# Eight-field to nine-field lookup and four-sample Gram products in a DLRM tower

## The reference

```python
combined = jnp.concatenate([dense_features[:, None, :], sparse_features], axis=1)
interactions = jnp.einsum('bfd,bgd->bfg', combined, combined)
iu, ju = jnp.triu_indices(27, k=1)
z = jnp.concatenate([dense_features, interactions[:, iu, ju]], axis=1)
h = jnp.concatenate([z, r_dense_features], axis=1)
h = jnp.maximum(h @ W_top1 + b_top1, 0.0)     # 607 -> 512
h = jnp.maximum(h @ W_top2 + b_top2, 0.0)     # 512 -> 256
y = h @ W_top3                                # 256 -> 1
```

## Time and profile before

| | before |
|---|---|
| median of 3 runs | 425.8 us (423.31 to 425.89) |
| span of the profiled execution | 704.5 us |
| mean granted TensorE clock in it | 0.741 |
| PE matmul busy | 384.2 us, 55% |
| DVE, ACT busy | 204.7 us, 135.2 us |
| POOL busy | 279.3 us, 40% |

### The profile page before, as it was taken

One profiled execution on the slowest core, in us unless ns is written; L12 is line 12 of the kernel. 1 busy time (PEld: TensorE's weight loads), 2 busy tenths in 40 slices (PEclk: granted clock), 3 DMA queues, 4 the chain that ended last, 5 costly groups with the idle time before them and its releaser, 6 DMA issues.

```text
span 704.5 us, 14426 instructions
## 1 busy us (share of the span) xinstructions
PE 384.2 (55%) x6049; PEld 340.9 (48%) x6049; DVE 204.7 (29%) x684; ACT 135.2 (19%) x265; POOL 279.3 (40%) x292
## 2 busy tenths in 40 slices
PE   0325428253727718295372954559364691648967
PEld 0325317152717707194361943449253581537856
DVE  0507227032304323062030710307112162304312
ACT  1104203021202202031120312114020231103421
POOL 6760452617370363605455053530727217270000
PEclk9957859775857958598585875759766696758987
DMA  4421422413023311133111331113302233013030
GB/s 135 161 84 67 130 68 60 115 40 81 22 56 55 94 53 27 48 68 92 34 30 45 68 96 30 45 34 69 102 20 54 44 75 87 23 53 54 24 46 17
DMA packets 43149, 44.14 MB, mean 63 GB/s; under 512 B 31028, under 2 KB 36028, under 8 KB 42126
## 3 DMA queue, kind: packets, MB, share of 16 engines
q1 hardware_dynamic: 33910, 24.91, 13.8%
q0 software_dynamic: 9216, 18.89, 10.9%
HBM read 38.12 MB, written 5.65 MB: 62 GB/s over the span
## 4 chain that ended last, share of the span: by engine, by line
PE 43%; issue 36%; DVE 6%; another core or an unknown queue 5%; SPq 3%; ACT 3%; DMA 3%; ACTq 0%; DVEq 0%
PE ps_g L339 13%; PE ps_o L314 13%; PE ps_m L353 11%; DVE onehot L647 5%; PE ps_t L325 4%; DMA h<-small_tables 2%; ACT emb L523 1%; SPq L258 1%; PE ps_m L380 1%; SPq L236 1%; ACT emb L514 1%; PE ps_o L397 1%; DMA x<-interaction_scratch 1%; DVE tbl_lo L638 1%
## 5 line engine op out<-in xcount | busy, mean ns | idle before, releaser
L287 POOL DMA_INDIRECT rows<-tables,idx x288 | 279.1, 969 | 355.0 <-DMA idx<-gather_ids 271.8
L647 DVE TENSOR_SCALAR onehot<-oh_ids,rownum 125x256 fp32r<-125x256 int32 x512 | 144.8, 357 | 318.1 <-PE ps_o L314 189.0
L339 PE MATMUL ps_g<-emb 128*32 128x27 f32 x4096 | 94.5, 209 | 199.0 <-issue 194.5
L339 PEld LDWEIGHTS ps_g<-emb 128*32 128x32 f32 x4096 | 70.9, 125 | 225.6 <-issue 220.5
L314 PE MATMUL ps_o<-onehot,tbl_hi 125*128 125x256 f32 x512 | 141.2, 310 | 66.1 <-DVE onehot L647 30.2
L314 PEld LDWEIGHTS ps_o<-onehot,tbl_hi 125*128 125x128 f32 x512 | 106.2, 207 | 73.2 <-issue 32.1
L314 PE MATMUL ps_o<-onehot,tbl_lo 125*128 125x256 f32 x512 | 135.0, 298 | 2.7 <-issue 2.7
L314 PEld LDWEIGHTS ps_o<-onehot,tbl_lo 125*128 125x128 f32 x512 | 106.3, 208 | 2.3 <-issue 2.3
L533 ACT ACTIVATE inter<-ps_g 128x432 f32<-128x432 f32 x32 | 17.0, 531 | 276.9 <-remote 157.6
L514 ACT ACTIVATE emb<-ps_o 128x256 f32<-128x256 f32 x64 | 38.9, 727 | 122.5 <-PE ps_o L314 83.5
L523 ACT ACTIVATE emb<-ps_t 128x512 f32<-128x512 f32 (+1 forms) x80 | 50.5, 664 | 46.3 <-remote 24.6
(11 more groups left out here) (53 smaller groups left out, 227.6 us busy)
## 6 DMA issues: line engine op xcount, KB each, us to landing
oh_ids<-onehot_ids SPq DMA_DIRECT2D x8, 1000.0 KB
rows<-tables,idx POOLq DMA_INDIRECT x288
interaction_scratch<-inter SPq DMA_DIRECT2D x32, 91.0 KB
x<-interaction_scratch SPq DMA_DIRECT2D x24, 117.0 KB
interaction_scratch<-inter SPq DMA_DIRECT2D x32, 81.2 KB
x<-small_tables SPq DMA_DIRECT2D x4, 500.0 KB
h<-small_tables SPq DMA_DIRECT2D x4, 500.0 KB
dense<-dense_t SPq DMA_DIRECT2D x8, 128.0 KB
```

The source lines that it names most:

```text
L287: pool.indirect_dma_start(rows[h][:, k, :], None, tables[k], bass.IndirectOffsetOnAxis(ap=idx[h][:, k:k + 1], axis=0),).then_inc(gathered[ ...
L339: mm = pe.matmul(ps_g[q][QROWS * j:QROWS * (j + 1), FEATURES * u:FEATURES * (u + 1)], emb[h][:, a:a + QROWS], emb[h][:, a:a + FEATURES], s ...
L647: op = nc.vector.tensor_scalar(onehot[k % 2][:, c, :], oh_ids[:, k, :], rownum[:, c:c + 1], None, ALU.is_equal)
```

## The change

- The Gram products take four samples at once: 108 stationary by 108 moving columns, of which the four 27x27 blocks on the diagonal are used. There are 64 such matmuls a block in place of 512; a PSUM bank holds four of them, so 16 copies of 108x432 a block take the place of 8 copies (four of 432, four of 208 columns). The wrapped columns are stored by DMAs of their own: 12 stores a block in place of 8.
- All ids of the gathers are loaded once at the start. A group of gathers waits only until the PE has turned the same group two halves before; there are two row buffers, as before.
- Nine fields are looked up and 17 gathered (groups of 4, 4, 4, 4, 1).
- The ids of the lookups are loaded field by field into a ring of five; the tables come through six staging buffers that lie in `inter`.
- The high parts of `x` and of layer 1's output are made by ACT, the low parts by DVE. Layer 3 has 2 matmuls of 256 columns in place of 4 of one column in 2 column halves, and the output is stored block by block.
- Loops are unrolled, and the order on PE, ACT and DVE is new: `layer1(m, 0)` stands behind four lookups, and all 16 banks of Gram products are at the end of the block.
- The scratch for GpSimd's DMA descriptors is set to 4096.

The core of the diff (the lines taken out of `body`, `grams`, `copy_grams` and `turn_interactions` can be read in the kernel above):

```diff
-ONEHOT = [3, 7, 9, 10, 11, 13, 15, 17]
+ONEHOT = [3, 7, 9, 10, 11, 13, 15, 17, 21]
...
+QUAD = 4
+QUADS = HALF // QUAD
+QCOLS = QUAD * FEATURES
...
-        idx = [sb(f"idx{h}", [128, NG], i32) for h in range(2)]
-        oh_ids = sb("oh_ids", [TPART, NO, BLOCK], i32)
-        rows = [sb(f"rows{h}", [128, NG, DIM]) for h in range(2)]
...
+        idx = sb("idx", [128, HALVES * NG], i32)
+        oh_ids = sb("oh_ids", [TPART, IDS, BLOCK], i32)
+        rows = [sb(f"rows{e}", [128, NG, DIM]) for e in range(2)]
+        emb = [sb(f"emb{e}", [128, HALF * FEATURES]) for e in range(2)]
...
-        inter = sb("inter", [128, WRAP, TB])
+        inter = sb("inter", [128, QCOLS, TB])
...
+        flat = inter[:, :, :].rearrange("p c t -> p (c t)")
+        stage = [flat[:, 1024 * s:1024 * (s + 1)] for s in range(6)]
+        stage += [t[:, :, :].rearrange("p c b -> p (c b)") for t in (x, h)]
+        TSTAGES = 6
...
+            def load_ids(n):
+                wait(sp, onehot_ready, n - IDS + 1)
+                i, k = divmod(n, NO)
+                sp.dma_start(oh_ids[:, n % IDS, :], src.to_broadcast([TPART, BLOCK])
+                             ).then_inc(ids_loaded[n % IDS], 16)
...
+                before = n - TSTAGES if n < NO else n - 2
+                if before >= (0 if n < NO else NO):
+                    sp.wait_ge(stage_split, before + 1)
+                sp.dma_start(stage[slot_of(n)][0:r, 0:w], src).then_inc(stage_loaded[slot_of(n)], 16)
...
+                sp.wait_ge(gram_copied, 2 * FILLS * (i + 1))
+                for j in range(QUAD):
+                    p, c = FEATURES * j, FEATURES * j
+                    sp.dma_start(scratch[0:BAND, 1:FEATURES, j, :],
+                                 inter[p:p + BAND, c + 1:c + FEATURES, :]
+                                 ).then_inc(inter_stored[0], 16)
+                for j in range(QUAD):
+                    p, c = FEATURES * j, FEATURES * j
+                    sp.dma_start(scratch[BAND:FEATURES, BAND + 1:FEATURES, j, :],
+                                 inter[p + BAND:p + FEATURES, c + BAND + 1:c + FEATURES, :]
+                                 ).then_inc(inter_stored[1], 16)
...
+            for i in range(1, BLOCKS):
+                turn_interactions(i - 1)
+                if i < LAST:
+                    load_dense(i + 1)
+                for n in range(NO * i + 7, min(NO * i + NO + 7, NO * BLOCKS)):
+                    load_ids(n)
+                if i >= 2:
+                    store_y(i - 2)
...
+            pool.wait_ge(idx_loaded, 16)
+            for hh in range(HALVES):
+                e = hh % 2
                 for g, (s, n) in enumerate(GROUPS):
-                    wait(pool, transposed, 2 * NGR * (i - 1) + NGR * h + g + 1)
+                    wait(pool, transposed, NGR * (hh - 2) + g + 1)
                     for k in range(s, s + n):
                         pool.indirect_dma_start(
+                            rows[e][:, k, :], None, tables[k],
+                            bass.IndirectOffsetOnAxis(ap=idx[:, NG * hh + k:NG * hh + k + 1], axis=0),
+                        ).then_inc(gathered[e][g], 16)
...
...
+            def grams(hh):
+                i, e = divmod(hh, 2)
+                pe.wait_ge(rows_placed, NGR * (hh + 1))
+                pe.wait_ge(onehot_placed, 2 * NU * (i + 1))
+                pe.wait_ge(dense_placed, hh + 1)
+                for b in range(FILLS):
+                    n = FILLS * hh + b
+                    wait(pe, gram_copied, n - 1)
+                    for u in range(BANK_QUADS):
+                        a = (BANK_QUADS * b + u) * QCOLS
+                        mm = pe.matmul(ps_g[n % 2][0:QCOLS, QCOLS * u:QCOLS * (u + 1)],
+                                       emb[e][:, a:a + QCOLS], emb[e][:, a:a + QCOLS],
+                                       start=True, stop=True)
+                    mm.then_inc(gram_done, 1)
...
+                for c in range(K2):
+                    mm = pe.matmul(ps_m[1][0:1, 0:BLOCK], w3s[:, c:c + 1], h2[:, c, :],
+                                   start=(c == 0), stop=(c == K2 - 1))
...
+            def body(i):
+                a, b, m = 2 * i, 2 * i + 1, i - 1
+                for k in range(4):
+                    lookup(i, k)
+                    transposes(a, k)
+                if i > 0:
+                    layer1(m, 0)
+                lookup(i, 4)
+                if i > 0:
+                    layer1(m, 1)
+                transposes(a, 4)
+                lookup(i, 5)
+                if i > 0:
+                    layer1(m, 2)
+                lookup(i, 6)
+                if i > 0:
+                    layer1(m, 3)
...
+                transposes(b, 0)
+                lookup(i, 7)
+                transposes(b, 1)
+                layer2(m, 0)
+                lookup(i, 8)
+                transposes(b, 2)
+                layer2(m, 1)
+                grams(a)
+                transposes(b, 3)
+                transposes(b, 4)
+                layer3(m)
+                grams(b)
...
+            def copy_grams(hh):
+                i, e = divmod(hh, 2)
+                if e == 0:
+                    wait(act, inter_stored[0], 16 * QUAD * i)
+                    wait(act, inter_stored[1], 16 * 2 * QUAD * i)
+                    if i == 0:
+                        act.wait_ge(stage_split, NO)
+                for b in range(FILLS):
+                    n = FILLS * hh + b
+                    act.wait_ge(gram_done, n + 1)
+                    src = ps_g[n % 2][0:QCOLS, 0:BANK_QUADS * QCOLS].rearrange("p (t c) -> p c t", c=QCOLS)
+                    t = QUADS * e + BANK_QUADS * b
+                    nc.scalar.activation(inter[0:QCOLS, :, t:t + BANK_QUADS], src, ACT.Copy
+                                         ).then_inc(gram_copied, 1)
+            def split_x_hi(m):
+                for c in X_ORDER:
+                    r = 128 if c == PAIR_CHUNKS else PAIR_ROWS
+                    act.wait_ge(x_loaded[c], 16 * (m + 1))
+                    if c == PAIR_CHUNKS:
+                        wait(act, l1_done, K1 * m)
+                    nc.scalar.activation(xr[0][0:r, c, :], x[0:r, c, :], ACT.Copy).then_inc(x_hi, 1)
+            def relu1(m, n, src):
+                wait(act, h1_split, K1 * m + n - 1)
+                if n == 0:
+                    wait(act, l2_done, K2 * m)
+                nc.scalar.activation(h1[:, n % 2, :], src, ACT.Relu, bias=b1s[:, n:n + 1]
+                                     ).then_inc(h1_ready, 1)
...
+            def body(i):
+                a, b, m = 2 * i, 2 * i + 1, i - 1
+                place_rows(a, 0)
+                place_rows(a, 1)
                 place_onehot(i, 0)
+                place_rows(a, 2)
+                split_x_hi(m)
+                place_rows(a, 3)
+                place_onehot(i, 1)
+                place_rows(a, 4)
+                relus1(m, 0)
+                place_onehot(i, 2)
+                place_rows(b, 0)
+                relus1(m, 1)
+                place_rows(b, 1)
+                place_onehot(i, 3)
+                place_rows(b, 2)
+                place_onehot(i, 4)
+                relus2(m)
+                copy_grams(a)
+                place_rows(b, 3)
+                place_rows(b, 4)
+                copy_grams(b)
...
+            def split_x_lo(m):
+                for k, c in enumerate(X_ORDER):
+                    r = 128 if c == PAIR_CHUNKS else PAIR_ROWS
+                    dve.wait_ge(x_hi, XCHUNKS * m + k + 1)
+                    nc.vector.tensor_tensor(xr[1][0:r, c, :], x[0:r, c, :],
+                                            xr[0][0:r, c, :].bitcast(f32), ALU.subtract
+                                            ).then_inc(x_split, 1)
...
             for k in range(NO):
                 split_lo(k)
+                make_onehot(k)
                 if k == 1:
                     place_dense(0)
+            make_onehot(NO)
+            make_onehot(NO + 1)
+            for n in range(NO, ITEMS):
                 split_lo(n)
+            for i in range(1, BLOCKS):
+                n = NO * i
+                make_onehot(n + 2)
                 place_dense(i)
+                make_onehot(n + 3)
+                split_x_lo(i - 1)
+                make_onehot(n + 4)
+                make_onehot(n + 5)
+                make_onehot(n + 6)
+                split_h1_lo(i - 1, (0, 1))
+                make_onehot(n + 7)
+                split_h1_lo(i - 1, (2, 3))
+                make_onehot(n + 8)
+                if i < LAST:
+                    make_onehot(n + 9)
+                    make_onehot(n + 10)
+                copy_y(i - 1)
...
-    nc = bacc.Bacc("TRN2", target_bir_lowering=False, num_devices=1)
+    nc = bacc.Bacc("TRN2", target_bir_lowering=False, num_devices=1, dynamic_dma_scratch_size=4096)
```

More of the change, by code:

```diff
@@ L318, in transposes, with lookup @@
-            def transposes(i, h, g):
-                s, n = GROUPS[g]
-                q = NGR * h + g
```

(24 more changed lines are left out.)

543 lines of the change are left out of this document (169 added, 374 removed).

## The result

| | before | after |
|---|---|---|
| median | 425.25 us (423.31 to 425.89, 4 runs) | 501.75 us (498.87 to 502.68, 4 runs) |
| ratio | | 1.181, 95% interval 1.176 to 1.186 |
| span of the profiled execution | 704.5 us | 499.5 us |

The account below looks back on a forecast made before the run. Gathers on POOL were taken to bound the kernel before (425.8 = 7 x 45.0 + 110.8). After the change the PE's cycle paces: 110.8 + 5 + 7 x 48.9 = 458 us, range 408 to 495.

Parts of the forecast that it names:

- Forecast block: Changed kernel's period between last Gram copies, chained through x's wait, lookups, layers and copies: 48.9 us, gathers (42.5) hidden.
- The fixed part: Start with block 0, tail and what lies around the span: 110.8 us before, plus 5 for the change.
- What bounds the kernel before: Gathers on POOL, one every 1.25 us, 36 a block, were said to set the pace at 45.0 us a block.
- The slack of 9 us: Room between the PE's 36 us of work a block and the gathers' 45.0 us in the kernel before.
- The check that gave 426 us: Third half's gathers at 77.95, 14 halves of 22.5 us, 28.0 us tail, about 5 us for last products; 425.8 measured.
- the "issue" time: 36% of the earlier trace's chain, 254 us, 194.5 of it in gaps between Gram matmuls; taken as the profiler's own.
- The new wait: PE waits for x in layer 1's first quarter, now behind four lookups, delaying lookup 4: 6.6 us a block.
- C: Start of the previous block's last Gram copy, from which the forecast timed a block; x's last piece at C + 14.7.
- The rival: PE clock halves after each new wait, adding 3.4 us a block: 482 us, chance 0.14.
- Gram matmuls at 0.10 us: 108x108 float32 products priced near a turned tile, 64 costing 6.4 us a block; copies pace at 0.57 us a bank.
- the other bound: Upper price of a 108-column Gram matmul, four times the strips' 42 ns: 0.168 us, giving +11 us.
- Ids of the gathers: POOL's id waits, of which the first, 28.2 us, had to be real, go in part; worth nothing since PE paces.

Follow-up runs that it names:

- b_unrolled: The kernel before with its five hardware loops written out and nothing else: 426.6 us, ratio 1.003.
- b_17gathers: The kernel before with the last of its 18 gathered fields left out, 34 gathers a block for 36, loops kept: 417.3 us, ratio 0.981.
- b_ids_once: The kernel before with all gather ids loaded once at the start and GpSimd's loop written out: 409.8 us, ratio 0.9635.
- a_strips: The changed kernel, its order kept, with the strip Gram products of the kernel before put back: 499.8 us, ratio 1.177.
- round 3: Third set of follow-up kernels, on the price of a Gram matmul, the gather ids and what paces a_order; the kernel before ran beside them.
- a_order: The changed kernel with layer 1's first quarter behind seven lookups again, and ACT's and DVE's splits moved to match: 438.3 us, ratio 1.027.
- a_fill: The changed kernel with 38 unused filler matmuls of 256 columns a block, around layer 1's first quarter and ahead of lookup 4: 489.9 us, ratio 1.151.
- a_gram_twice: The changed kernel with each Gram matmul issued twice, 128 more a block: 593.4 us.
- a_onepass: The changed kernel with the features kept as float32r, so Gram products use rounded features: 497.3 us.
- a_onepass_order_fill1: a_onepass_order with one unused 256-column filler matmul behind each bank's four Gram matmuls: 416.3 us, ratio 0.981.
- a_onepass_order: The changed kernel with the order of a_order and the rounded float32r features of a_onepass: 434.8 us, ratio 1.021.
- a_order_ids: a_order with two lookup-id loads a block (fields 7 and 8) issued between the stores and loads of x's turn-around: 442.8 us, ratio 1.041.

## Why the prediction was too low

Forecast block 48.9 us, measured 55.1 to 55.2. The fixed part comes out: 7 x 48.9 + 115.8 was the sum, 501.75 - 7 x 55.16 is 115.6. That is in part luck. By the same measure the mean block of b_unrolled is 43.7 us (ends of the Gram products at 92.6 and 398.6), not 45.0, since the other engines start late and catch up with the gathers; its fixed part is then some 120.5. So start and tail became some 5 us shorter, where the forecast had them 5 longer from a base that was 10 too low.

- *What bounds the kernel before: right.* Gathers at 1.25 us pace it (b_unrolled, b_17gathers, b_ids_once). The slack of 9 us below them was too much: after 1 us a block another bound takes over. The check that gave 426 us hit by luck: in b_unrolled the third half's gathers start at 65.69 and not at 77.95, the 14 halves take 323 us and not 315, and 10 us and not 5 lie between the last gather and the last Gram copy. The reason that I gave for the 704.5 us, that each small product leaves its own records, is wrong: a_strips has as many and a span of 496.9, b_17gathers has the loops too and 417.7. Nor is that one execution alone: one of the 11 runs of the kernel before that stood beside round 3 took 573.76 us, at a granted clock of 1.00, where the others took 422.7 to 426.1. What stretches an execution so stays open. To set the "issue" time aside was right all the same.
- *The new wait: right, and most of the change.* x at C + 14.6 and lookup 4 at C + 18.0 are the forecast to 0.1 us. With the order changed back (a_order) 63.5 of 76 us return, some 12 of which are the clock's (a_fill).
- *A step that failed: the clock, put at nothing.* The rival was true, and I gave it 0.14, because lookups stood around the gap and 12 matmuls in it. They don't keep it up. Its size was 3.4 us a block in the rival; the stretched instructions sum to 2.4 to 2.6, and holding the clock up is worth 12 us in all.
- *The step that failed most: Gram matmuls at 0.10 us, with the copies as the bound.* A float32 matmul of 108 columns costs 0.177 us and 0.12 a bank, 0.207 on average, and a half takes 6.6 us for 4.5. The PE sets the pace of the stage, and ACT waits for it. I took the turned tile as the nearer shape, but that leaves one record where a float32 product leaves two; the other bound, four times the strip's 42 ns, was 0.168. The strip products of before were miscounted as well: a block has 256, one a sample, and not 512; they leave 512 records, and I took the records for products (the section on the change has the same error). Had I scaled records and not products (four samples, two records each of 10.5 ns, times four for the width) the upper end would have been 0.336. So it is luck that 0.168 lies near 0.177. The Trainium skill's TensorEngine Tiling (Array Packing), Performance Considerations, recommends column tiling by four for operands of this size; the traces agree with the direction only: by sample the strips cost 28 ns against 52 without their gaps, a factor of 1.9, and 35 against 53 with them, 1.5.
- *The sum.* On the forecast's own scale from C, the first Gram copy starts at 41.4 for 39.1, the eighth at 47.0 for 42.9, the last at 55.2 for 48.9. Of the 6.3 us a block, 44 us in all, by which the forecast was short, 2.3 come ahead of the Gram stage, where the stretch at half clock stands, and 4.0 in it. Either alone would have left the time inside the range (an estimate from the forecast: 474 and 486 us). Layer 3 took 0.95 us for 0.3, but between the two halves, where it stands, the copies pause for 2.5 us against 2.1 in the forecast, so little of that counts.
- *Why no edit found those 4 us alone.* Put back as strips the products cost gaps and a later x; made cheap as one record each they leave the PE idle and the clock falls. Only with the clock held up and x off the path do they show: 438.3 to 416.3, 3.1 us a block, down to where the gathers are.
- *Ids of the gathers: right for the changed kernel, and missed as an edit.* In the order of before it is worth 15 us. That it is worth nothing where the PE waits for x was not run by itself; in after GpSimd waits 77 us for the PE, so earlier ids could hardly help. The real wait ahead of the third half was 15.0 us and not the 28.2 of the earlier trace rows.

What stays open: the gaps of 1 to 3 us in strip products, the shares of the chains in a_order's 46 us, and what stretches single executions of the kernel before.

## What to carry to other kernels

A result that goes out through DRAM and comes back has a turn-around (here 14.6 us) that is one loop with everything that stands between its use and its next making: place the first use behind more work than that, and count what queues on each engine behind it. Where an engine falls idle in the new order, price the work behind the gap at the lower clock, and price a cheaper instruction likewise: in a stage paced by another engine it may give nothing until filler matmuls close the gap. And try the small edits of a big change one by one: here one of them, alone, made the kernel 3.6% faster, inside a change that made it 18% slower.

## What the runs showed of the hardware

- A float32 matmul of 108x108 leaves two records and costs 0.177 us at the full granted clock (a_gram_twice). With float32r operands it leaves one record and costs 0.20 us at the half clock (a_onepass); at the full clock four of them and a 256-column matmul fit in 0.60 us (a_onepass_order_fill1).
- The granted clock fell to 0.50 after stretches in which the PE was busy 1.1 of 4.5 us (after), and also in a stage where it was busy 1.85 of 2.7 (a_onepass_order). In the same stretches with 38 filler matmuls a block (a_fill), or with one a bank (a_onepass_order_fill1), it stayed at 1.00. More instructions made the kernel faster, by 12 and by 18.5 us.
- The last of three x loads took 6.9 us from issue to landing behind two 125 KB loads of lookup ids (a_order_ids), for 3.6 without them (after).
- One profiled execution of the kernel before was 1.65 times as long as the median of its runs, and one timed run 1.35 times (573.76 us); a kernel with the same loops and the same number of small matmuls (b_17gathers) had a span of 417.7.
